# Grouped attention: both rounds with V at the end of a slot, the ring's pieces in pairs ahead of them

## The reference

```python
x = x + _L0_attn_ref(_layernorm(x, axis=-1), ...)   # differential attention
x = x + _L0_ffn_ref(_layernorm(x, axis=-1), ...)    # grouped attention, then 8 experts, top 2
x = x + _L1_attn_ref(_layernorm(x, axis=-1), ...)   # 8 linear-attention blocks
x = x + _L1_ffn_ref(_layernorm(x, axis=-1), ...)    # ternary MLP

# in _L0_ffn_ref
h = _rmsnorm(hidden_states, ln1_w)
q = _apply_rope((h @ Wq).reshape(b, s, H, HD), cos, sin)
k = _apply_rope((h @ Wk).reshape(b, s, HKV, HD), cos, sin)
v = (h @ Wv).reshape(b, s, HKV, HD)
scores = jnp.einsum('bqhd,bkhd->bhqk', q, k) / np.sqrt(HD).astype(np.float32)
scores = jnp.where(causal[None, None], scores, jnp.finfo(scores.dtype).min)
attn = jax.nn.softmax(scores, axis=-1)
ctx = jnp.einsum('bhqk,bkhd->bqhd', attn, v).reshape(b, s, H * HD)
h = jnp.clip(residual + ctx @ Wo, -100.0, 100.0)
```

## Time and profile before

| what | value |
|---|---|
| median of 3 runs | 3207.44 us (3206.28 to 3207.7) |
| span of the profiled execution, first to last instruction | 3203.1 us |
| what the runs have around that span | 3.2 to 4.6 us |
| PE, PEld busy | 2943.1 us (92%), 1857.9 us (58%) |
| DVE, ACT, POOL busy | 2466.5 (77%), 2325.1 (73%), 2092.1 us (65%) |
| mean granted TensorE clock over the span | 0.956 of full speed |
| score and maximum pieces of the grouped attention | from 535.6 to 1302.6 us |

### The profile page before, as it was taken

The page is one execution under the profiler, slowest core; times in us unless marked ns, Lnnn a source line. Parts: engine busy times, 40 slices in busy tenths (PEclk is TensorE's granted clock), DMA queues, the critical chain, the costliest instruction groups (busy, mean ns, idle before and its releaser), DMA issues. The chain is left out here.

```text
span 3203.1 us, 66211 instructions
## 1 busy us (share of the span) xinstructions
PE 2943.1 (92%) x22258; PEld 1857.9 (58%) x22258; DVE 2466.5 (77%) x6944; ACT 2325.1 (73%) x3601; POOL 2092.1 (65%) x2402
## 2 busy tenths in 40 slices
PE   6999997788898898789579999999999999999979
PEld 3555554344444444578446666666666666666658
DVE  5666665888787776468468888888888888888867
ACT  5777874465565566544279999999999999999933
POOL 5566664345555563477657887887887887887744
PEclk8999998799898999899879999999999999999989
DMA  4534434222222211386400000000000000000001
GB/s 120 129 101 116 118 96 95 58 62 67 61 53 67 67 48 43 117 280 185 149 15 1 17 1 7 11 6 12 1 17 1 17 1 16 1 13 4 1 14 40
DMA packets 151509, 178.31 MB, mean 56 GB/s; under 512 B 18619, under 2 KB 122784, under 8 KB 151076
## 3 DMA queue, kind: packets, MB, share of 16 engines
q1 hardware_dynamic: 142084, 157.14, 18.9%
q0 software_dynamic: 9088, 16.94, 1.5%
HBM read 99.82 MB, written 75.95 MB: 55 GB/s over the span
## 5 line engine op out<-in xcount | busy, mean ns | idle before, releaser
L3372 PE MATMUL lb_FF<-lb_h,lb_w 128*128 128x512 f32 x1024 | 501.2, 592 | 0.0
L3601 DVE TENSOR_SCALAR lb_z<-lb_M,lb_mv,lb_rstd 128x128 f32<-128x128 f32 x1024 | 344.9, 399 | 3.3 <-POOL lb_rstd L3526 3.0
L3489 ACT ACTIVATE lb_h<-lb_H,lb_prm 128x512 f32<-128x512 f32 x512 | 326.6, 697 | 2.6 <-PE lb_H L3363 2.6
L3526 POOL TENSOR_TENSOR lb_rstd<-lb_rstd,half 128x4 f32<-128x4 f32 x256 | 260.4, 1017 | 37.2 <-issue 1.3
L3357 PE MATMUL lb_H<-lb_x1s,lb_w 128*128 128x512 f32 x512 | 272.2, 532 | 0.8 <-issue 0.8
L3372 PEld LDWEIGHTS lb_FF<-lb_h,lb_w 128*128 128x128 f32 x1024 | 193.5, 189 | 89.5 <-issue 61.0
L544 ACT ACTIVATE ga_PT<-ga_S 128x384 f32<-128x384 f32 x256 | 111.7, 489 | 183.2 <-PE ga_S L355 183.2
L1570 ACT ACTIVATE da_PT<-da_SY 128x1536 f32<-128x1536 f32 x128 | 185.2, 1447 | 72.2 <-PE da_SY L1419 72.0
L3593 DVE BATCH_NORM_STATS2 lb_stats<-lb_M 128x6 f32<-128x128 f32 x1024 | 227.2, 284 | 13.1 <-PE lb_M L3316 7.9
L1648 POOL TENSOR_SCALAR_AFFINE_SELECT da_PT<-da_PT 128x1024 f32<-128x1024 f32 x128 | 141.4, 1110 | 132.4 <-ACT da_PT L1565 132.4
L3358 PE MATMUL lb_H<-lb_x1s,lb_w 128*128 128x512 f32 x512 | 203.0, 397 | 0.0
(11 more groups left out here) (514 smaller groups left out, 8851.9 us busy)
## 6 DMA issues: line engine op xcount, KB each, us to landing
moe_w<-experts_dram SPq DMA_DIRECT2D x39, 384.0 KB, 3.3
da_qT<-da_stq SPq DMA_DIRECT2D x64, 192.0 KB, 4.0
da_kT<-da_stk SPq DMA_DIRECT2D x64, 192.0 KB, 3.6
moe_x<-moe_xs SPq DMA_DIRECT2D x39, 260.0 KB, 3.7
tc_g<-moe_ys SPq DMA_DIRECT2D x32, 256.0 KB, 4.3
ga_q<-ga_stq SPq DMA_DIRECT2D x20, 384.0 KB, 6.1
lb_split<-moe_parts SPq DMA_DIRECT2D x8, 896.0 KB, 6.5
da_stq<-da_parts SPq DMA_DIRECT2D x16, 384.0 KB, 2.4
```

Source lines behind the costliest of these rows:

```text
L3372: pe.matmul(FF[:, :], w2[:, k, :], h[:, k, :], start=(k == 0), stop=(k == KC - 1)).then_inc(ff_filled, 1)
L3489: act.activation(h[:, k, :], H[:, k % 2, :], ACT.Gelu_apprx_tanh, bias=col(FB1 + k, i)).then_inc(h_ready, 1)
L3526: pool.tensor_tensor(out[:, :], out[:, :], C["half"][:, 0:NT], ALU.pow).then_inc(done, 1)
L3601: last = v.tensor_scalar(z[:, t, :], M[:, t * P:(t + 1) * P], mv[:, t, 0:1], rstd[:, t:t + 1], ALU.subtract, ALU.mult)
```

## The change

Nothing is computed differently; three orders change. On PE `max_scores(m, 0)` and `score(n, 1)` move ahead of the first shared use, and both rounds with V move behind the second shared use. On ACT `exponentials(n, 2)` follows `exponentials(n, 1)` directly. On DVE `take_max(m, 0)` comes first in the slot, and `take_max(m, 2)` follows `take_max(m, 1)` directly, ahead of the reader of the second shared use. No semaphore, tile or size changes.

```diff
 # pe_program
                     if attending:
                         score(n, 0)
+                    if scanning:
+                        max_scores(m, 0)
+                    if attending:
+                        score(n, 1)
                     if s == 0 and exists(p):
                         turn_o(p, 2)
...
                     if scanning:
-                        max_scores(m, 0)
-                    if weighing and s % 2 == 0:
-                        pe.wait_ge(probs, 6 * group + 6)
-                        if group:
-                            pe.wait_ge(o_copied, group)
-                        weigh(group, FIRST[0])
-                    if weighing and s % 2 == 1:
-                        weigh(group, SECOND[0])
+                        max_scores(m, 1)
                     if attending:
-                        score(n, 1)
+                        score(n, 2)
                     if scanning:
-                        max_scores(m, 1)
+                        max_scores(m, 2)
                     if s == 0 and exists(c2):
                         sum_k(c2)
...
-                    if attending:
-                        score(n, 2)
-                    if scanning:
-                        max_scores(m, 2)
+                    if weighing and s % 2 == 0:
+                        pe.wait_ge(probs, 6 * group + 6)
+                        if group:
+                            pe.wait_ge(o_copied, group)
+                        weigh(group, FIRST[0])
+                    if weighing and s % 2 == 1:
+                        weigh(group, SECOND[0])
                     if weighing and s % 2 == 0:
                         weigh(group, FIRST[1])
 # act_program
                     if attending:
                         exponentials(n, 1)
+                        exponentials(n, 2)
                     if s == 0 and exists(c2):
                         copy_sum(c2)
...
-                    if attending:
-                        exponentials(n, 2)
 # dve_program
+                    if scanning:
+                        take_max(m, 0)
                     if s == 0 and exists(p):
                         combine(p, 2)
...
                     if scanning:
-                        take_max(m, 0)
+                        take_max(m, 1)
                     if scanning:
-                        take_max(m, 1)
+                        take_max(m, 2)
                     if s == 0 and exists(c2):
                         split_q(c2)
...
-                    if scanning:
-                        take_max(m, 2)
                     if s == 0 and exists(c2):
                         split_k(c2)
```

## The result

The change makes the kernel a little slower: median 3219.93 us (3219.34 to 3224.05, 5 runs) against 3206.28 (3204.66 to 3207.7, 5 runs), ratio 1.0045 with a 95% interval of 1.0033 to 1.0057. The forecast was 3230, with 3195 to 3260 for 8 in 10. The profiled executions differ by 15.1 us, 3218.2 against 3203.1, at the same mean clock of 0.956.

The account below looks back on a forecast made before the run. It took PE's own work to bound half of each block and DVE slots 1 to 4; 10 x (-0.1 + 2.0) + 4 x (-0.1) + 4 = +22.6 on the 3203.1 span gives 3226, measured 3230, 8 in 10 within 3195 to 3260.

Parts of the forecast that it names:

- the signs listed: Trace signs: PE idle ahead of max2 in slots 6, 7, 0; one slot 1 gap near 1.9; low clock once a block.
- The floor of a slot: In each slot, waits for ACT and DVE keep max2 from starting before t + 2.83 and score2 before t + 2.49.
- Slots 5, 6, 7, 0: PE-bound slots: moved work no longer overlaps the waits; +1.5 us a block together, between nothing and +3.
- Slots 1 to 4: DVE-bound slots: DVE's 2.03 wait is filled; 24.8 us instead of 26.4, -1.6 a block with the clock up.
- The clock: PE's gaps in slots 1 and 4: clock falls once in 10 of some 14 blocks, costing 2.0 us each.
- Rival two: Slots 4 and 5 drop the clock again, or each slot's wait keeps it low: +59, 3266 us; chance 0.18.
- The rival in which the clock stays up: Clock stays up if slot 1's gap stays under some 1.6: -3 to -10, about 3200 us; chance 0.25.
- The tail: Eleven slots without maxima: score2 waits for score0's exponentials, 0.3 to 0.4 us each, +4 (0 to 8).

Follow-up runs that it names:

- e3: The changed kernel with the first round with V put back between max1 and score2, the second left at the end; 0.9940 of the kernel before.
- e4: The changed kernel with six overwritten bf16 matmuls ahead of score2 in each of slots 1 and 4; 0.9957 of the kernel before.
- e7: The kernel before with five overwritten matmuls ahead of score1 in slot 1, its first gap; 0.9993 of the kernel before.
- e1: The kernel before with only ACT's and DVE's new orders, PE in the old one; 1.0057 of the kernel before.
- e8: The changed kernel run again with no edit; 1.0053 of the kernel before.
- e5: e3 with split_k moved ahead of split_q on DVE in slot 0; 0.9893 of the kernel before.

## Why the prediction was right, and where its terms were off

The sign and the waits behind it held, and the size was 7.5 us too large: +22.6 predicted on the span, +15.1 seen, of which 11.4 in the stage. Of the signs listed, two did not come: slot 7 has no wait ahead of max2, and the clock falls twice in most blocks and not once. By the steps:

*The floor of a slot* held. max2 starts 2.85 after slot 6, forecast 2.83, and score2 2.39 after slots 5 and 6 (951.04 - 948.65, 956.15 - 953.76), forecast 2.49. e3 shows the cause: with one round with V between max1 and score2 the waits are gone. They come in four slots of a block (40 in ten blocks): 3, 5, 6 and 0. In slot 7, which the prediction named as well, `project_qs` keeps PE at work, and max2 starts 2.85 after the slot without a wait.

*Slots 5, 6, 7, 0*: +1.5 a block forecast, 21.24 - 20.63 = +0.6 measured in the block shown (5.11, 5.54, 5.13, 5.46 against 4.47, 5.59, 5.17, 5.40) and +0.8 on the mean of eleven, where slot 5 takes 5.29; with the clock up, in e4, it takes 5.11 in every one. This is one of two mis-sized terms. The prediction carried both rounds with V over with the steps that they had apart. Before:

```profile
944.38 0.39 PE L355 MATMUL ga_S<-ga_q,ga_k 51*128 51x384 bf16 x4
...
946.23 0.42 PE L388 MATMUL ga_O<-ga_PT,ga_v 128*32 128x128 f32 x8
```

From the rounds' starts to the next instructions that is 0.78 (943.60 to 944.38) and 0.36 (946.23 to 946.59), 1.14 together; one behind the other they take 1.00 (952.76 to 953.76). The other three slots save as much (1.57 to 1.42 in slot 6, 1.57 to 1.43 in slot 0, 1.15 to 1.00 in slot 7): together some 0.6 of the 0.9 a block that the forecast was too high. Why two rounds in a row take less is not shown. Slot 5 gained 0.2 more because `copy_max` moved the exponentials of score1 by 0.49 (950.30 to 950.79) and not by 0.68. In slots 6 and 0 the free `turn_o`, which had waited 0.37 and 0.26, pays for the waits ahead of score2 and max2, 0.2 each.

*Slots 1 to 4*: 24.8 forecast with the clock up, and e4, with the clock nearly always up, has 24.98; 26.8 forecast with one fall, and the mean is 26.78 (26.58 before). The filled DVE wait and the single gap came as put. The gap of 2.30 against 1.9 is 0.1 of a later start of `split_q` (0.77 ahead of slot 1, not 0.9) and 0.2 more for `split_k`, told below; slot 4's is 1.81 against 1.6.

*The clock*: "falling once" was the wrong count and, by luck, the right price. Rival two had the count: slot 4's gap drops it too. But I took each fall's price from the kernel before, where it lasts 7 us; here the two last 3.5 each, so a block is low about as long as before. e4 gives the price with the clock nearly always up: 24.3 us over the stage, 2.0 a block (48.20 against 46.22), where 2.0 were taken for ten of 14 blocks. Of the gaps of slots 1 and 4, 2.30 and 1.81 in the block shown, one or both are followed by a fall in every block; the new waits of 0.17 to 0.64 us in slots 5 and 6 dropped nothing (clock 1.00 from 935 to 975). Whether the change loses against the kernel before by the clock is not shown: the mean is 0.92 in both, and what the falls cost in the old order no run measured, as e7 did not take them away.

The rival in which the clock stays up (3200) was refuted for the change as it stands. Nor does a gap under some 1.6, which was the author's estimate, decide it by itself: in its order e1's single gap of 1.33 was followed by a fall in eight blocks of ten. e4 shows what the rival would have been: 3193.39, with 1.0 us a block gained (46.22 against 47.19), the upper end of the 0.5 to 1.0 of its sum; it lies below the rival's 3200 because the tail did not cost 4. The second round with V directly behind the first did not keep the clock up either: the mean is 0.92 in both kernels.

*The tail*: +4 forecast, -2.1 measured, wrong in sign and the other mis-sized term. (From the first mask of the first slot without maxima, 1259.25 before and 1271.82 after, to the last mask it is 39.7 and 36.5, -3.2; the part up to it is then +14.6.) I counted score2's new wait (0.34 of it seen) and left out that `turn_o` had stood between mask and V, waiting 1.30 and, in the next even slot, 1.48 for O's copy, and again the 0.15 that two rounds in a row save in a slot. Before, and then after:

```profile
1268.55 0.63 PE L259 MATMUL ga_M<-ident,ga_oT 128*128 128x128 f32 x4 [1.30 <-ACT ga_oT L505]
```

```profile
1280.68 0.39 PE L355 MATMUL ga_S<-ga_q,ga_k 51*128 51x384 bf16 x4 [0.34 <-ACT ga_PT L545]
1281.73 0.63 PE L259 MATMUL ga_M<-ident,ga_oT 128*128 128x128 f32 x4 [0.66 <-ACT ga_oT L505]
```

That these are the whole of the tail's gain is argued from such rows, not tried by itself.

So the sum: +13.5 up to the last scan where 18.6 were forecast, -2.1 in the tail where +4 were. Together the two errors are 11 us. The 3.7 outside the stage, which bring the result nearer to the forecast, stay unexplained; e8's 2.0 suggest that they vary from execution to execution. Why the clock falls for 3.5 us in the one order and for 7 in the other stays open too.

## What to carry to other kernels

In a ring of PSUM banks between one producer and several readers, the producer's order and each reader's order are one decision: the same two edits cost 4.2% and 0.6% alone and 0.45% together, so cost them as a pair, walking the ring piece by piece. Work that waits for nothing belongs between the pieces whose banks are still being read, not behind the last one; moving one of the two rounds back was worth 31 us of stage, and filling a reader's wait with independent work (`split_k`) another 17.5, the clock's share in it included. What a gap costs through the clock is told by a version with overwritten matmuls in it: 24 us for 0.06 of mean clock in one order here; in another, 5 us for 0.02, too little to be told from nothing. And a step carried over from a trace holds for the neighbours that it had there: two rounds with V here take 0.15 us less in a row than apart.

## What the runs showed of the hardware

Two of DVE's operations from SBUF, both of `split_k`, took longer when they started beside a GpSimd operation: the 32x512 subtraction 1.49 us instead of 0.68, the 32x512 cast 0.99 instead of 0.41. The view of single lines, all fifteen sequences, before:

```profile
L771 DVE TENSOR_TENSOR ga_restK<-ga_restK,ga_partsK x15: 678/680/681, 561.9 to 1204.3; 32x512 f32<-32x512 f32 x15
...
L769 DVE CAST ga_partsK<-ga_restK x15: 946/992/1000, 560.8 to 1203.3; 32x512 bf16<-32x512 f32 x15
```

and after:

```profile
L770 DVE TENSOR_TENSOR ga_restK<-ga_restK,ga_partsK x15: 1482/1491/1494, 559.3 to 1213.8; 32x512 f32<-32x512 f32 x15
...
L768 DVE CAST ga_partsK<-ga_restK x15: 406/406/408, 558.8 to 1213.3; 32x512 bf16<-32x512 f32 x15
```

The change put the reduce of max2 ahead of `split_q`, so `split_k` comes one short step earlier against POOL's `third_q`: the subtraction and not the cast now starts beside it, and grows by 0.81 us while the cast shrinks by 0.59, with POOL's operation 0.1 longer (1.15 before, 1.26 after). The subtraction ends 0.55 after POOL's operation (923.26 + 1.26 = 924.52, 923.58 + 1.49 = 925.07), 0.13 less than the 0.68 that it takes alone, as if it had begun just ahead of that end. The cast does the same before:

```profile
919.46 0.99 DVE L769 CAST ga_partsK<-ga_restK 32x512 bf16<-32x512 f32 x1
```

It ends 0.28 after POOL's operation (919.02 + 1.15 = 920.17, 919.46 + 0.99 = 920.45), 0.13 less than the 0.41 that such a cast takes alone (L773 at 921.28, with POOL idle from 920.17 to 921.77). In e5, where the cast starts while the rotation runs, the cast is the long one again (1.07) and the subtraction takes 0.68. No run here varied the neighbour on POOL alone, and why the two stretch is not shown.
